# First expert layer of a two-layer transformer kernel: the second bias moves from a TensorE product into VectorE's weighting step, with a new written-out order

## The reference, cut to what matters

```python
logits = xf @ Wr + br
topv, _ = lax.top_k(logits, TOPK)
masked = jnp.where(logits >= topv[:, TOPK - 1:TOPK], logits, -jnp.inf)
weights = jax.nn.softmax(masked, axis=-1)
h = jax.nn.gelu(jnp.einsum('td,edh->eth', xf, W1) + b1[:, None, :], approximate=False)
expert_out = jnp.einsum('eth,ehd->etd', h, W2) + b2[:, None, :]
out = jnp.einsum('etd,te->td', expert_out, weights)
```

## Time and profile before

| | us |
|---|---|
| median of 3 runs (572.86 to 574.75) | 574.48 |
| the profiled execution, own time | 574.52 |
| its span, first to last instruction | 572.7 |
| PE busy (share of span) | 556.3 (97%) |
| DVE busy | 447.4 (78%) |
| ACT busy | 376.1 (66%) |
| POOL busy | 170.1 (30%) |

### The profile page before, as it was taken

One profiled execution on the slowest core, in us unless ns is written; L12 is line 12 of the kernel. 1 busy time (PEld: TensorE's weight loads), 2 busy tenths in 40 slices (PEclk: granted clock), 3 DMA queues, 4 the chain that ended last, 5 costly groups with the idle time before them and its releaser, 6 DMA issues.

```text
span 572.7 us, 8759 instructions
## 1 busy us (share of the span) xinstructions
PE 556.3 (97%) x2677; PEld 393.5 (69%) x2677; DVE 447.4 (78%) x1343; ACT 376.1 (66%) x663; POOL 170.1 (30%) x173
## 2 busy tenths in 40 slices
PE   7898999999999999999999999999999999999996
PEld 7565566665777667767677667677776766677885
DVE  6988999792555656877868787988988999879794
ACT  2576677768766787856976589873765532475553
POOL 4101120011242212163113324137012031455574
PEclk9999999999999999999999999999999999999998
DMA  4401000401111110111101111341221231432540
GB/s 137 186 19 29 1 9 2 148 1 38 56 38 38 38 47 19 38 38 40 69 31 37 58 36 38 106 147 57 92 92 68 99 98 64 146 110 84 158 146 24
DMA packets 23328, 38.42 MB, mean 67 GB/s; under 512 B 3792, under 2 KB 9552, under 8 KB 22896
## 3 DMA queue, kind: packets, MB, share of 16 engines
q1 hardware_dynamic: 22848, 37.44, 20.1%
q10 hardware_dynamic: 432, 0.40, 0.2%
HBM read 36.45 MB, written 1.38 MB: 66 GB/s over the span
## 4 chain that ended last, share of the span: by engine, by line
PE 86%; DVE 6%; ACT 3%; issue 2%; POOL 1%; DMA 1%; POOLq 0%; SPq 0%; ACTq 0%; DVEq 0%
PE ps L1640 11%; PE ps L1642 10%; PE ps L1641 10%; PE ps L1863 8%; PE ps L2036 5%; PE ps L1652 4%; PE ps L1739 4%; PE ps L1653 3%; PE ps L1654 3%; PE ps L1759 3%; PE ps L1635 3%; PE ps L1647 2%; PE ps L1773 2%; PE ps L1776 2%; PE ps L1940 2%
## 5 line engine op out<-in xcount | busy, mean ns | idle before, releaser
L1640 PE MATMUL ps<-xThi,w1s 128*128 128x512 f32 x256 | 122.5, 479 | 1.3 <-DVE h L1591 0.6
L999 ACT ACTIVATE h<-ps,early 128x512 f32<-128x512 f32 x128 | 86.1, 686 | 47.5 <-PE ps L1642 25.1
L1642 PE MATMUL ps<-xTlo,w1s 128*128 128x512 f32 x256 | 100.8, 394 | 0.0
L1641 PE MATMUL ps<-xThi,w1s 128*128 128x512 f32 x256 | 100.5, 393 | 0.0
L1130 ACT ACTIVATE s<-ps 128x512 f32<-128x512 f32 x68 | 40.7, 598 | 62.8 <-PE ps L1642 62.3
L862 POOL TENSOR_TENSOR acc_o<-acc_o,ty 128x512 f32<-128x512 f32 x32 | 43.6, 1361 | 85.1 <-DVE ty L1391 80.0
L1640 PEld LDWEIGHTS ps<-xThi,w1s 128*128 128x128 f32 x256 | 48.2, 188 | 26.3 <-issue 7.8
L1863 PE MATMUL ps<-h,w2s 128*128 128x512 f32 x128 | 65.8, 596 | 0.3 <-DVE ty L1391 0.3
L1295 DVE TENSOR_REDUCE NM<-ps 128x2 f32<-128x308 f32 x128 | 55.9, 471 | 5.5 <-PE ps L1739 3.8
L1352 DVE TENSOR_TENSOR h_r<-h,s_r 128x512 fp32r<-128x512 f32 x64 | 48.1, 752 | 14.7 <-ACT s_r L885 14.5
L1591 DVE TENSOR_TENSOR h<-s,ps 128x512 f32<-128x512 f32 x68 | 46.4, 682 | 15.7 <-PE ps L1642 12.0
(11 more groups left out here) (293 smaller groups left out, 1156.0 us busy)
## 6 DMA issues: line engine op xcount, KB each, us to landing
CB<-ct_rows SPq DMA_DIRECT2D x128, 128.0 KB, 2.9
WB<-wt_rows SPq DMA_DIRECT2D x32, 256.0 KB, 3.3
w2s<-w_dram SPq DMA_DIRECT2D x2, 2048.0 KB, 9.3
raw<-gu_dram SPq DMA_DIRECT2D x4, 512.0 KB, 4.1
x_in<-x_dram SPq DMA_DIRECT2D x4, 256.0 KB, 3.0
w2s<-dn_dram SPq DMA_DIRECT2D x1, 1024.0 KB, 4.7
out_dram<-ty SPq DMA_DIRECT2D x3, 256.0 KB, 3.0
late<-late_dram SPq DMA_DIRECT2D x1, 608.5 KB, 7.8
```

Of the source, the lines that this page charges most:

```text
L999: nc.scalar.activation(h32[:, c % HR, :], bank[c % 2], ACT.Gelu, bias=b1T[:, c:c + 1]).then_inc(b_gelu.sem, 1)
L1640: M(dst, w[0], xThi[:, x, :], start=start, stop=False)
L1641: M(dst, w[1], xThi[:, x, :], start=False, stop=False)
L1642: return M(dst, w[0], xTlo[:, x, :], start=False, stop=stop)
```

## The change: what it does

The four bias products and their four copies go. In their place TensorE transposes `b2dup` once (128x128), ScalarE copies 8 columns of the result to a new tile `b2T` (128 features by 8 experts), and VectorE's step for each expert becomes (bank 2 + column e of `b2T`) * `WB` in one instruction. Expert 0 writes straight to `acc_o`, so GpSimd adds 7 terms in place of 8 for each batch element. The memset of `WT` shrinks from 1024 to 128 columns, and all order tables are written anew.

```diff
+    def term(b, e):
+
+        return b * (E0 - 1) + e - 1
...
-            for e in range(E0):
+            for e in range(1, E0):
                 yield
                 pool.wait_ge(b_ty.sem, b_ty.at(b, e + 1))
-                if e:
-                    pool.wait_ge(b_acc.sem, b_acc.at(b, e))
-                else:
-                    pool.wait_ge(b_base.sem, b_base.at(b, 1))
-                nc.gpsimd.tensor_tensor(acc_o[:], acc_o[:], ty[:, e % 2, :], ALU.add).then_inc(b_acc.sem, 1)
+                if e > 1:
+                    pool.wait_ge(b_acc.sem, b_acc.at(b, e - 1))
+                nc.gpsimd.tensor_tensor(acc_o[:], acc_o[:], ty[:, term(b, e) % 2, :], ALU.add).then_inc(b_acc.sem, 1)
...
-        def base(b):
-            yield
-            act.wait_ge(b_base_ps.sem, b_base_ps.at(b, 1))
-            if b:
-                act.wait_ge(b_o_ps.sem, b_o_ps.at(b, 0))
-            else:
-                act.wait_ge(a_y_ps.sem, a_y_ps.at(NB - 1, 1))
-            copy(acc_o[:], bank[3]).then_inc(b_base.sem, 1)
+        def base():
+            yield
+            act.wait_ge(b_base_ps.sem, b_base_ps.at(0, 1))
+            copy(b2T[:], bank[3][:, 0:E0]).then_inc(b_base.sem, 1)
...
-            V.memset(WT[:], 0.0).then_inc(pads.sem, 1)
+            V.memset(WT[:, 0, 0:P], 0.0).then_inc(pads.sem, 1)
...
-                if b * E0 + e >= 2:
-                    dve.wait_ge(b_acc.sem, b_acc.at(b, e - 1))
-                V.tensor_tensor(ty[:, e % 2, :], bank[2], WB[:, e % 2, :], ALU.mult).then_inc(b_ty.sem, 1)
+                if e:
+                    if term(b, e) >= 2:
+                        dve.wait_ge(b_acc.sem, b_acc.at(b, e - 2))
+                elif b:
+                    dve.wait_ge(b_o_ps.sem, b_o_ps.at(b, 0))
+                else:
+                    dve.wait_ge(a_y_ps.sem, a_y_ps.at(NB - 1, 1))
+                    dve.wait_ge(b_base.sem, b_base.at(0, 1))
+                dst = ty[:, term(b, e) % 2, :] if e else acc_o[:]
+                V.scalar_tensor_tensor(dst, bank[2], b2T[:, e:e + 1], WB[:, e % 2, :], ALU.add, ALU.mult).then_inc(b_ty.sem, 1)
...
-        def weights(b):
-            yield
-            pe.wait_ge(b_wt.sem, b_wt.at(b, 1))
+        def weights():
+
+            yield
+            pe.wait_ge(early_loaded.sem, 48)
             claim(3)
-            M(bank[3], b2dup, WT[:, b % 2, :], start=True, stop=True).then_inc(b_base_ps.sem, 1)
-            read_by(3, b_base, b_base.at(b, 1))
+            nc.tensor.transpose(bank[3][:, 0:P], b2dup, ident).then_inc(b_base_ps.sem, 1)
+            read_by(3, b_base, b_base.at(0, 1))
```

One line of each of two tables, for what the new order looks like in the code:

```diff
-    "weights": [[13311], [19016], [25875], [32779]],
+    "weights": [[13372]],
-    "stage_b": [[15115, 15251, 16010, 16183, 16692, 17279, 18070, 18529], [19722, 20480, 21349, 22407, 23805, 24001,
+    "stage_b": [[15007, 15478, 16271, 16849, 17436, 18000, 18590], [20339, 21294, 22230, 22798, 23768, 24821, 24956],
```

More of the change, by code:

```diff
@@ new lines @@
+    "biased": [[923], [2537], [3245], [6006]],
+    "split0": [[3953, 4660, 5614, 6952, 7038, 9115, 9175, 10145]],
+    "maxima": [[1560, 1598, 1658, 1696, 1768, 1806, 1861, 1900, 1950, 1969], [1984, 2022, 2075, 2115, 2167, 2205, 2259,
[9 rows of a table added]
+    "normalise": [[3663, 3825, 3852], [4892, 4917, 4936], [6446, 6501, 6520], [7782, 7807, 7827], [9651, 9676, 9696],
+        [10621, 10682, 10740], [12362, 12387, 12406], [13320, 13345, 13365]],
+    "output": [[5295], [8254], [11077], [13862]],
+    "norm_b": [[5770, 6066, 8061, 9109, 9235, 10205, 10224, 10352], [11178, 11431, 11657, 11955, 12913, 13647, 13666,
+        13922], [14860, 14951, 15650, 15668, 16259, 17612, 17988, 18151], [19391, 19481, 22195, 22214, 22430, 26122,
+        26494, 26545]],
@@ L286 @@
-    "context_keys": [[720], [1556], [4747], [7756]],
-    "context_values": [[824], [4364], [7107], [10148]],
-    "inputs": [[899, 1037], [2378, 2881], [5134, 5740], [8194, 8351]],
-    "queries": [[1378, 1688, 1944, 3066], [3982, 4795, 4911, 5921], [6824, 7619, 8000, 8836], [9516, 10473, 10861,
-        11662]],
-    "keys": [[1148, 1257], [3559, 3748], [6595, 7300], [8919, 9419]],
-    "maxima": [[1525, 1539, 1625, 1664, 1732, 1756, 1827, 1866], [1919, 1988, 2048, 2080, 2133, 2184, 2229, 2276],
[7 rows of a table removed]
@@ L310 @@
-    "prepare_b": [[10641, 11519, 12824], [15687, 17325, 18503], [19336, 21013, 23741], [27123, 27562, 31110]],
-    "first": [[12729, 13169, 13459, 13620, 13688, 13850, 13918, 14214, 14282, 14509, 14732, 14801, 15028, 15096, 15320,
[8 rows of a table removed]
-    "weights": [[13311], [19016], [25875], [32779]],
-    "second": [[13534, 13990, 14059, 14145, 14354, 14440, 14578, 14664, 14873, 14959, 15165, 15251, 15460, 15730,
[8 rows of a table removed]
-    "stage_c": [[16103, 17503, 19260, 19380, 19633, 19719], [25964, 26040, 26224, 26310], [32364, 32733, 32868, 32954]
-        , [38731, 39465, 39738, 39893]],
@@ new lines @@
+    "context_keys": [[734], [1557], [4680], [7820]],
+    "context_values": [[781], [4248], [7143], [10090]],
+    "inputs": [[899, 1037], [2485, 2740], [5498, 5760], [8098, 8310]],
+    "queries": [[1380, 1768, 1937, 3016], [3822, 4775, 4865, 5942], [6872, 7615, 8001, 8793], [9521, 10467, 10637,
+        11679]],
+    "keys": [[1148, 1230], [3485, 3776], [6491, 6635], [8913, 9447]],
+    "maxima": [[1518, 1540, 1624, 1649, 1715, 1752, 1818, 1862], [1912, 1980, 2041, 2073, 2125, 2169, 2217, 2262],
[7 rows of a table added]
@@ new lines @@
+    "prepare_b": [[10874, 11390, 13157], [14278, 14772, 18495], [18928, 20526, 24458], [26883, 27264, 30199]],
+    "first": [[12839, 13300, 13452, 13520, 13681, 13842, 14138, 14206, 14479, 14548, 14861, 14930, 15243, 15380, 15449,
[8 rows of a table added]
+    "weights": [[13372]],
+    "second": [[13595, 13914, 13983, 14069, 14325, 14411, 14617, 14703, 15002, 15088, 15157, 15311, 15520, 15744,
[8 rows of a table added]
+    "stage_c": [[16186, 17857, 18851, 19421, 19605, 19691], [25624, 25838, 26039, 26125], [32471, 32547, 32695, 32781]
+        , [38342, 39285, 39490, 39576]],
@@ new lines @@
+    "scores_c": [[19781, 19892, 20227, 20292], [26218, 26329, 26664, 27020], [32873, 32896, 33231, 33562], [39961,
+        40120, 40318, 40383]],
+    "turns_c": [[20515, 20863, 21026, 21426], [26800, 26998, 27580, 27891], [33414, 33741, 34241, 34390], [40698,
+        41022, 41132, 41460]],
+    "attends_c": [[20956, 20979, 21470, 21606], [27685, 27776, 27821, 28023], [33834, 34343, 34503, 34570], [41644,
+        41667, 41712, 41919]],
+    "cross": [[21902, 22243, 22728, 22772, 23307, 24713, 24966, 25373], [28388, 28730, 29283, 29327, 29794, 31096,
+        31590, 31860], [34886, 35297, 36111, 36154, 36395, 37468, 37649, 38122], [42146, 42592, 43604, 43648, 44162,
+        45634, 45815, 46485]],
@@ L1143, in _ @@
                ("group", [group(b, g) for b in every for g in range(NG)]), ("output", map(output, every)),
[L1144 removed]
+               ("prepare_b", map(prepare_b, every)), ("base", [base()]), ("gelus", map(gelus, every)),
                ("split1", [split1()]), ("split2", [split2()]), ("split3", [split3()]), ("highs_b", map(highs_b, every)),
@@ L2065, in _ @@
                ("values", [values(b, g) for b in every for g in range(NG)]), ("output", map(output, every)),
-               ("prepare_b", map(prepare_b, every)), ("first", map(first, every)), ("weights", map(weights, every)),
+               ("prepare_b", map(prepare_b, every)), ("first", map(first, every)), ("weights", [weights()]),
                ("second", map(second, every)), ("stage_c", map(stage_c, every)), ("scores_c", map(scores_c, every)), ("turns_c", map(turns_c, every)),
```

229 lines of the change are left out of this document (105 added, 124 removed), and 198 rows, old and new, of tables (PLAN_ACT, PLAN_DVE, PLAN_PE, PLAN_SP).

## The result

The changed kernel takes 568.63 us (median of 4 runs, 568.38 to 568.83) against 574.3 us for the kernel before on the same chip (median of 4, 572.86 to 574.75). The ratio is 0.9904, with a 95% interval of 0.9888 to 0.992: 1.0% faster, 5.5 us by the ratio (5.7 by the medians). The forecast was 571.4 with a range from 569.0. The profiled execution has a span of 567.0 us and took 568.83.

The account below looks back on a forecast made before the run. Behind 138.2 us TensorE's own work was taken to set the end. Sum: 574.52 - 3.44 (bias products) + 0.11 (transpose) + 0.2 (VectorE) = 571.4 us, everything else at 0; range 569.0 to 574.5.

Parts of the forecast that it names:

- Bias products, 3.44 us: TensorE behind 138.2 us: four removed products at 0.86 us each count in full, 2.58 us of it for elements 1 to 3.
- rival A: TensorE's saved work is handed back to waits on other engines, near 7 us: 573 to 575, no measurable change; chance 0.20.
- The new order, counted at 0: Fresh interleaving of all steps, stage a included: middle 0, allowing 2 us won or 3 us of new waits.
- rival C: Stage a's reordered round trips between TensorE and VectorE lose 4.8 us through 13 more waits: 576.2 or more; chance 0.08.
- this case: Stated condition for a wrong prediction: stage a ends more than a microsecond off its old 138.2 us for like work.
- Rival B: The new order also removes half of the second part's 4.3 us of TensorE waits: 569.3; chance 0.16.
- VectorE, +0.2: New step takes 748 ns, +56 ns each; TensorE sees it at three or four hand-overs of bank 2, costing 0.2 us.
- rival D: The column makes VectorE's step contend with GpSimd, a long tail delaying bank 2 hand-overs: 574 to 575; chance 0.06.
- Transpose: The one new transpose on TensorE costs 0.11 us.
- ScalarE, GpSimd: Four 0.59 us copies become one of 8 columns, and four 1.29 us additions go: both counted at nothing.
- Memset: Start of program: shorter memset counted at 0, upper bound 0.5 us; 16 idle products would end at 8.6 us.
- The way to `WB`: Element 0's later `WT` copy: `WB` there at 145.7 to 146.9 us, first step about 146.8; nothing, at most 1 us.

Follow-up runs that it names:

- experiment 10: Kernel before, its four bias products, copies and additions kept, in the whole new order, element 1's product one block later than first placed: 571.81 us, ratio 0.9961.
- experiment 5: The changed kernel once more, unaltered, beside the kernel before on its chip: 568.14 us, ratio 0.9901.
- experiment 1: The changed code with the order tables of the kernel before, slots of dropped steps taken out: 573.77 us, ratio 1.0005.
- experiment 8: The changed code with the new order for stage a alone and the old order behind it: 572.01 us, ratio 0.9974.
- experiment 9: Kernel before with the new order for stage a alone, but the copy of `WT` put back ahead of the Gelus: 572.71 us, ratio 0.9975.
- experiment 13: Changed kernel, new order for stage a's first 36 us and behind 138 us, old order for the rest of stage a: 568.26 us, ratio 0.9901.
- experiment 14: Changed kernel with the old order for stage a's first 36 us and the new order for all behind: 570.57 us, ratio 0.9937.
- experiment 11: Changed kernel with stage a's old order, only its 24 idle products at the new order's places: 570.79 us, ratio 0.9934.
- experiment 4: Changed kernel with VectorE's new step as a plain multiplication without the column, second bias left out: 567.88 us, ratio 0.9903.
- experiment 12: Changed kernel with the memset of `WT` over all 1024 columns again: 568.34 us, ratio 0.9901.
- experiment 2: Kernel before with the new order for stage a alone, the copy of `WT` behind the Gelus: 574.02 us, ratio 1.0016.
- experiment 7: Changed code in the old order, one later block moved into each of the four removed products' places: 573.82 us, ratio 1.0009.
- experiment 3: Changed kernel with the old order for stage a and the new order behind 138 us: 569.73 us, ratio 0.9937.

## Why the prediction was wrong in size

**Bias products, 3.44 us.** The size came out for the kernel as it was changed: 3.4 us (experiment 10 against 5) and 3.7 us of the rest (434.4 less 430.7). But the ground given was wrong, so this was in part luck. "For elements 1 to 3 they stand in a row of back-to-back products, ... so that part, 2.58 us, should come out whole" would hold in the old order too, and there it is worth nothing (experiments 1, 8 against 9). That was rival A, and it had its mechanism nearly right: TensorE arrives early where others set the pace. Its sign, waits near 7 us, came true in experiment 1 with 6.5. What I missed is that a product in such a row may itself be what hides the next wait, as I had seen it for element 0 alone. I had looked at the row and not at whether the instruction behind it had its operand yet.

**The new order, counted at 0 ("Middle: 0").** This is the step that failed. The order was not neutral: it is worth 2.2 us even with the products in (experiment 10, ratio 0.9961), of which 1.4 us lie in stage a (experiment 9, 0.9975), and without it the 3.44 us would not have come out at all. For the changed code stage a's share is 2.1 us (0.9937 to 0.9901). I looked for a win only among the second part's waits, whose sum did not shrink, and saw stage a only as a risk (rival C), although its 14.1 us of waits for VectorE were the largest entry among TensorE's waits. Experiments 13 and 14 put the win into the first 36 us, and in the first 40 us these waits fell from 5.9 to 2.0 us; 11 rules out the idle products by themselves. Which of the other steps there wins it was not tried and stays open. The prediction had named this case as what would make it wrong: stage a ending more than a microsecond off.

**Rival B** (the order also wins, 569.3) had the right sign and came near by number, but through the second part's waits, whose sum did not shrink. The measured parts, 574.3 - 3.4 - 2.2 = 568.7, meet the 568.63, but this is no check of them: both are differences to the same experiment 10.

**VectorE, +0.2.** The duration was exact, 748 ns, and rival D's tail did not appear; the cost at the end is somewhere from 0 to 0.75 us by what experiments 4 and 5 show. That the step does not stretch beside GpSimd is seen in the changed kernel's timeline, where GpSimd's two additions run from 380.62 us on. The new step, with its column and one tensor in SBUF, takes its usual 0.75 us under them, and the two `h_r` steps behind it, with two operands in SBUF, take 1.02 and 1.32 us in place of their median of 0.68 (timeline: start, duration, engine):

```profile
380.62 2.97 POOL L864 TENSOR_TENSOR acc_o<-acc_o,ty 128x512 f32<-128x512 f32 x2
380.75 0.75 DVE L1395 SCALAR_TENSOR_TENSOR ty<-ps,b2T,WB 128x512 f32<-128x512 f32 x1 [1.46 <-PE ps L1658]
381.41 1.02 DVE L1350 TENSOR_TENSOR h_r<-h,s_r 128x512 fp32r<-128x512 f32 x1
382.81 1.32 DVE L1350 TENSOR_TENSOR h_r<-h,s_r 128x512 fp32r<-128x512 f32 x1 [0.38 <-ACT s_r L887]
```

The Trainium skill's page DVE: scalar operands, raw-bit mode, write accounting and state across instructions, section Scalar operands, says that a per-partition scalar operand does not take up the second tensor stream. These rows agree. **Transpose** (0.11), **ScalarE, GpSimd** at nothing: nothing in the traces speaks against it; they were not tried by themselves. **Memset** 0: right (experiment 12), though the 16 idle products did not last until 8.6 us; they ended at about 6.7, since 32 instructions took 5.50 us. **The way to `WB`**: in time. By the old times `WB` was to be there at 145.7 us at the earliest and the first step to run at 146.8; stage a ended 1.8 us earlier, and the step ran at 144.95 without a wait for the DMA. But the same late copy would have cost the old code its whole win in stage a (experiments 2 and 9): in the changed kernel nothing on TensorE reads `WT` there any more.

**The base of the sum.** The profiled execution of before carried losses of its own, the low clock at its end and one in stage a. A small DMA of stage a was issued in 1.84 us instead of the usual 0.43 (median 426 ns), and VectorE, and with it TensorE for 1.2 us, waited for it:

```profile
46.69 1.84 SPq L694 DMA_DIRECT2D mask<-mask_dram  x1
```

```profile
50.69 0.17 DVE L1191 CAST mk<-mask 128x2 f32<-128x2 uint8 x1 [1.25 <-DMA mask<-mask_dram]
```

The late issue looks like chance (it is in seven of the sixteen profiled executions, with either order), but what it costs hangs on the order. In the old stage a VectorE takes this mask 3 to 4 us after the start of its issue, and issues of 1.84, 1.36 and 1.33 us made it wait 1.25, 0.76 and 0.72 us (before, experiments 11 and 7). In the changed kernel the issue was late too, 1.16 us, but VectorE takes the mask 11 us after it, and waited for nothing. So of the 1.9 us between the two shown traces in stage a a part is this wait. It is not what sets the medians: experiment 13 takes the mask as early as the old order and has the whole win.

## What to carry to other kernels

A product in a back-to-back row on a 97% busy TensorE is worth its time only if the instruction behind it has its operands earlier. Look in the trace when the next operand was ready, instruction by instruction, before counting a removed one in full. An edit that takes work out and a new order are best priced as a pair, by a two-by-two table: here neither won much behind the seam, and both together won about 4 us. And where the waits are is where a new order can win, be it far from the edit.

## What was not expected of the hardware

In several executions with the old order of the first 36 us TensorE's granted clock fell to its lower level, 1.2 GHz, at about 20 us, after a microsecond in which TensorE had been busy 0.7 to 0.8 of the time. The windows of experiment 1's kernel (us, busy time of the engines, clock, DMA), and a row of the same stretch in experiment 3's, whose order is the same up to there and whose TensorE had been busy the same 0.72 of the microsecond ahead:

```profile
19.00:20.00 1.00, 0.72 (x3) 0.33 (x3) 1.00 (x4) 0.00 (x0) 0.00 (x0) 0.94 0.94 360
20.00:21.00 1.00, 1.00 (x4) 0.99 (x5) 1.00 (x7) 0.00 (x0) 0.00 (x0) 0.50 0.57 197
21.00:22.00 1.00, 1.00 (x7) 0.99 (x6) 0.37 (x2) 0.53 (x1) 0.00 (x0) 0.50 0.13 44
22.00:23.00 1.00, 1.00 (x5) 0.68 (x3) 0.37 (x2) 0.49 (x2) 0.00 (x0) 0.50 0.04 12
```

```profile
20.00:21.00 1.00, 1.00 (x9) 1.00 (x10) 1.00 (x8) 0.24 (x1) 0.00 (x0) 1.00 0.98 329
```

It cost 1.3 us within the next 6 us (the transposes of `xn` at 25.84 against 24.49 us, started 0.07 us apart), and it appeared in three of six profiled executions with these steps in the old order (experiments 1, 7 and 14, not in before, 3 and 11), in none of the ten with the new one; but two of those (4 and 5) had a fall at 11 to 14 us, and experiment 2 the one at 139 us. In experiment 1 the five runs with a mean clock of 0.997 have a median of 574.46 us and the four with 1.0 one of 573.16. By these counts the fall is perhaps a part of the new order's win in the first 36 us, but not all of it: in experiment 14 the three executions with a mean clock of 0.997 have spans of 568.6 to 568.8 us and the other three 567.6 to 567.9, against 566.1 to 566.6 in experiment 13. And the traces of experiments 3 and 13, neither of which has a fall or a late mask issue, still differ by 0.9 us at `OZ`.
